# A cross-attention's values taken two units at a time, and the weight differences of an FFN moved beside the next attention's output products

## The reference

```python
# cross-attention, 16 heads, latents of width 32
C_q = Q @ Wq_d; C_kv = K @ Wkv_d
CqWqk = (C_q @ W_qk).reshape(b, n, H, LKV)
scores = einsum('bnhl,bkl->bhnk', CqWqk, C_kv) / sqrt(LKV)
attn = softmax(scores); V_up = (C_kv @ Wv_u).reshape(b, nkv, H, HD)
out = einsum('bhnk,bkhd->bnhd', attn, V_up)
# grouped attention: 32 heads of 128, 8 key heads, 16 blocks of 32 cached keys + 64 new ones
# FFN with weights in two values around a mean: for each of w1, w2, w3
d = w - base; coeff = mean(abs(d)); W = base + coeff * sign(d)
h = silu(x @ W1.T) * (x @ W3.T); out = h @ W2.T
x = x + xattn(ln(x)); x = x + attn(ln(x)); x = x + ffn(ln(x))
```

## Time and profile before

| | us |
|---|---|
| median of 3 runs | 906.02 (902.95 to 907.76) |
| the profiled execution | 903.59 |
| its span, first to last instruction | 901.8 |
| cross-attention's loop over contexts | 45.2 to 285.4 |
| rotated keys | 287.8 to 315.7 |
| grouped attention and FFN | from 317.6 |
| a group of the attention | 56.2 |
| busy: PE, DVE, ACT, POOL | 861.6, 609.3, 521.6, 416.4 |

### The profile page before, as it was taken

One profiled execution on the slowest core, in us unless ns is written; L12 is line 12 of the kernel. 1 busy time (PEld: TensorE's weight loads), 2 busy tenths in 40 slices (PEclk: granted clock), 3 DMA queues, 4 the chain that ended last, 5 costly groups with the idle time before them and its releaser, 6 DMA issues.

```text
span 901.8 us, 15515 instructions
## 1 busy us (share of the span) xinstructions
PE 861.6 (96%) x5402; PEld 654.4 (73%) x5402; DVE 609.3 (68%) x994; ACT 521.6 (58%) x1011; POOL 416.4 (46%) x272
## 2 busy tenths in 40 slices
PE   6899999999987979999999999999999999899998
PEld 4445555555532768888888888888888887788886
DVE  4865676577543448768587685876858769767784
ACT  4756666666675546546365463654636557555552
POOL 2597787778874024423244232442324525144430
PEclk9989999999998989999999999999999999999999
DMA  9947756532651522011020110201102004446521
GB/s 358 325 169 273 275 209 213 192 127 66 217 174 59 222 83 71 24 41 54 0 70 23 43 50 0 70 23 40 53 0 70 13 1 137 144 141 204 188 99 47
DMA packets 43202, 102.96 MB, mean 114 GB/s; under 512 B 7954, under 2 KB 13074, under 8 KB 42258
## 3 DMA queue, kind: packets, MB, share of 16 engines
q1 hardware_dynamic: 42866, 102.06, 33.0%
q10 hardware_dynamic: 288, 0.26, 0.1%
HBM read 96.95 MB, written 1.05 MB: 109 GB/s over the span
## 4 chain that ended last, share of the span: by engine, by line
PE 61%; DVE 2%; ACT 1%; DMA 1%; POOL 0%; SPq 0%; issue 0%
PE psum L1359 11%; PE psum L1345 10%; PE psum L1475 9%; PE psum L1413 8%; PE psum L1371 6%; PE psum L1489 4%; PE psum L1398 3%; PE psum L1389 3%; PE psum L1394 3%; PE psum L1380 1%; PE psum L1392 1%; PE psum L1390 1%; DMA ffn_raw<-in_L_ffn_mean_w_dram 1%; POOL ffn_quant L1860 0%; DVE x L1831 0%; DVE norm_stats L162 0%
## 5 line engine op out<-in xcount | busy, mean ns | idle before, releaser
L1847 POOL TENSOR_TENSOR head_probs<-head_probs,inverse_den 128x576 f32<-128x576 f32 x128 | 147.4, 1152 | 273.1 <-DVE inverse_den L1700 273.0
L982 DVE TENSOR_REDUCE max_part<-psum 128x1 f32<-128x804 f32 x128 | 121.0, 989 | 44.0 <-PE psum L694 43.9
L871 ACT ACTIVATE probs<-psum 128x512 f32<-128x512 f32 (+1 forms) x208 | 107.9, 601 | 54.7 <-PE psum L715 48.1
L1582 ACT ACTIVATE head_probs<-psum,neg_max 128x576 f32<-128x576 f32 x128 | 94.8, 741 | 51.1 <-DVE neg_max L1713 50.4
L555 POOL TENSOR_TENSOR prob_sums<-probs 128x1024 f32<-128x1024 f32 x48 | 114.2, 2389 | 18.7 <-ACT probs L871 9.8
L1713 DVE TENSOR_REDUCE neg_max<-psum 128x1 f32<-128x576 f32 x128 | 96.9, 757 | 23.8 <-PE psum L1359 22.6
L1359 PE MATMUL psum<-k_high,query_t_high 128*128 (+1 forms) x256 | 86.6, 338 | 2.0 <-DVE coeff L1786 2.0
L1693 DVE TENSOR_TENSOR probs_t_low<-psum,probs_t_high 128x512 fp32r<-128x512 f32 x124 | 84.8, 684 | 1.0
L715 PE MATMUL psum<-q_t,c_t 97*128 97x512 f32 (+1 forms) x208 | 73.7, 435 | 7.9 <-ACT probs L871 6.3
L1371 PE MATMUL psum<-ident,head_probs 128*128 128x128 f32 x496 | 77.9, 273 | 1.6 <-DVE query_t_low L1672 1.4
L694 PEld LDWEIGHTS psum<-c_t,q_t 96*128 96x128 f32 x256 | 43.6, 190 | 47.9 <-DVE max_part L982 25.1
(11 more groups left out here) (221 smaller groups left out, 1919.3 us busy)
## 6 DMA issues: line engine op xcount, KB each, us to landing
ctx_t_odd<-in_ctx_dram SPq DMA_DIRECT2D x4, 3202.0 KB, 10.7
w_raw<-in_L_ffn_w_dram SPq DMA_DIRECT2D x24, 448.0 KB, 5.1
w_raw<-in_L_ffn_mean_w_dram SPq DMA_DIRECT2D x24, 448.0 KB, 6.4
ffn_raw<-in_L_ffn_w_dram SPq DMA_DIRECT2D x42, 256.0 KB, 3.8
ffn_raw<-in_L_ffn_mean_w_dram SPq DMA_DIRECT2D x42, 256.0 KB, 4.3
cache<-in_ctx_dram SPq DMA_DIRECT2D x3, 3202.0 KB, 10.8
wq_nat<-in_L_attn_wq_dram SPq DMA_DIRECT2D x32, 256.0 KB, 3.0
wo_nat<-in_L_attn_wo_dram SPq DMA_DIRECT2D x32, 256.0 KB, 2.7
```

The costliest lines, as they stand in the source:

```text
L871: act.activation(prob_buffer(b, t)[0:rows, half * BANK:(half + 1) * BANK], psum[0:rows, n % SCORE_BANKS, :], ACT.Exp, scale=XSCALE).then_i ...
L982: dve.tensor_reduce(max_part[:, qt, pair:pair + 1], psum[:, bank:bank + 2, 0:PIECE_KEYS], AX.XY, ALU.max).then_inc(s_max, 1)
L1582: act.activation(probs[:, qt, :].rearrange("p (a k) -> p a k", a=2), psum[:, 2 * (qt % 2):2 * (qt % 2) + 2, 0:HALF], ACT.Exp, bias=neg_max ...
L1847: pool.tensor_tensor(probs[:, qt, :], probs[:, qt, :], rden[:, qt:qt + 1].to_broadcast([P, KEYS]), ALU.mult).then_inc(s["norm"], 1)
```

## The change

- The ring `probs` has eight tiles instead of four. `values` takes two units in one visit (16 records), so there are three visits of full tiles per context instead of six, after the scores of tiles 5, 9 and 12.
- Instead of six pair sums there are three sums of four or five tiles in contexts 0 to 4 (`STEADY`), five in contexts 5 and 6, and five sums and two single tiles in context 7. GpSimd adds tile by tile, ten additions a context in the first form. The tail's values are made in the same round as the denominators of the first sum, after the next context's first two tiles of scores.
- Maxima 14 and 15 follow the last visit of values, ahead of the compression and the turn of the maxima. Maximum 1 comes behind the scores of tile 3.
- The differences for `coeff` leave cross-attention. In the grouped attention, each group g from 1 to 7 handles a seventh of each matrix (1024 columns): six loads of 512 KB issued on SyncE's queue in its iteration for g, three differences on GpSimd in head (g, 0) behind the copy of the values, three absolute sums on ScalarE in head (g, 0) behind `output_weight_high(g, 0)`, one small addition on GpSimd in head (g, 1). The product that spreads the sums, and `coeff`, move into head (7, 2). `difference(0)` moves ahead of the first head.

```diff
-PIECE = WSIZE // P // BATCH
+PIECE = WSIZE // P // (NKV - 1)
...
+STEADY = ((0, 1, 2, 3), (4, 5, 6, 7), (8, 9, 10, 11, 12))
+FEWER = ((0, 1, 2), (3, 4, 5), (6, 7), (8, 9), (10, 11, 12))
+FEWEST = ((0, 1, 2), (3, 4), (5, 6), (7, 8), (9, 10), (11,), (12,))
+GROUPED = (STEADY,) * (BATCH - 3) + (FEWER, FEWER, FEWEST)
...
-            def add_pair(b, u):
...
+            def add_tile(b, t, n, first):
+
+                rows = slice(0, rows_of(t))
+                total = sum_buffer(b, n)
+                pool.wait_ge(s_exp, HALVES * b + 2 * t + 2)
+                if first:
+                    wait(pool, s_den, sum_freed(b, n))
+                else:
+                    pool.wait_ge(s_add, adds_through(b, t) - 1)
+                pool.tensor_tensor(total[rows, :], (prob_buffer(b, t - 1) if first else total)[rows, :],
+                                   prob_buffer(b, t)[rows, :], ALU.add).then_inc(s_add, 1)
...
+            def values(b, units):
+
+                pe.wait_ge(s_exp, HALVES * b + 2 * tiles_of(units[-1])[-1] + 2)
+                if units[0] == 0:
+                    pe.wait_ge(s_cnat, b + 1)
+                    wait(pe, s_u, 2 * b)
+                for u in units:
+                    for half in range(2):
+                        cols = slice(half * BANK, (half + 1) * BANK)
+                        for odd, t in enumerate(tiles_of(u)):
+                            at = 2 * LKV * half + LKV * odd
+                            mm = pe.matmul(psum[at:at + LKV, U_BANK, :], c_nat[:, b % 3, t, :],
+                                           prob_buffer(b, t)[:, cols], start=(u == 0), stop=(t + 2 >= KT))
...
+                pe.wait_ge(s_exp, HALVES * (b + 1))
+                pe.wait_ge(s_add, adds_through(b, parts[0][-1]))
+                for half in range(2):
+                    at = 2 * LKV * half
+                    mm = pe.matmul(psum[at:at + LKV, U_BANK, :], c_nat[0:TAIL, b % 3, KT - 1, :],
+                                   prob_buffer(b, KT - 1)[0:TAIL, half * BANK:(half + 1) * BANK], start=False, stop=True)
+                    add_up(0, 1, half)
+                mm.then_inc(s_pv, 1)
+                for n in range(1, len(parts), 2):
+                    wait(pe, s_add, adds_through(b, parts[n + 1][-1]))
                     for half in range(2):
...
+                maximum(0)
+                scores(b, 2)
+                if b == 0:
+                    maximum(1)
+                    compress(2)
+                scores(b, 3)
+                if b > 0:
+                    maximum(1)
+                    mix(b - 1)
+                maximum(2)
+                if b == 0:
+                    natural(2)
+                scores(b, 4)
+                maximum(3)
+                scores(b, 5)
+                maximum(4)
+                values(b, range(0, 2))
+                for t in range(6, 10):
+                    maximum(t - 1)
+                    scores(b, t)
+                maximum(9)
+                values(b, range(2, 4))
+                for t in range(10, KT):
+                    maximum(t)
+                    scores(b, t)
+                maximum(KT)
+                values(b, range(4, 6))
+                maximum(KT + 1)
+                maximum(KT + 2)
                 if b + 3 < BATCH:
                     compress(b + 3)
                 if lead:
                     turn_max(b + 1)
-                values(b, UNITS - 1)
                 if b + 3 < BATCH:
                     natural(b + 3)
                 if lead:
                     scores(b + 1, 0)
                     scores(b + 1, 1)
-                denominators(b)
+                tail_and_denominators(b)
```

In the grouped attention, SyncE's loop over g:

```diff
+                    if i == 1:
+                        sp.wait_ge(s_abs, 3 * (g - 1) + 1)
+                        for k in range(3):
+                            for j, n in enumerate(wnames[k]):
+                                sp.dma_start(pieces[k][:, j, :], flat[n][:, bass.ds((g - 1) * PIECE, PIECE)]
+                                             ).then_inc(s_piece[k], 16)
```

TensorE, in `score`, and ahead of the first head:

```diff
+                if isinstance(g, int) and n == NH - 2 and qt == 1:
+                    pe.wait_ge(s_tot, NKV)
+                    pe.matmul(psum[:, 3, HALF:HALF + 3], ones[:, :], total[:, :], start=True, stop=True).then_inc(s_all, 1)
+                elif isinstance(g, int) and n == NH - 2 and qt == 3:
+                    pe.wait_ge(s_co, 1)
...
-            pe.wait_ge(s_ones, 1)
-            pe.wait_ge(s_tot, 1)
-            pe.matmul(psum[:, 7, 0:3], ones[:, :], total[:, :], start=True, stop=True).then_inc(s_all, 1)
-            pe.wait_ge(s_co, 1)
             run(pe, head)
```

ScalarE, at the end of `head`:

```diff
                 if this and i == 0:
                     output_weight_high(g, i)
+                if last and i == 0:
+                    for k in range(3):
+                        abs_sum(g, k)
+
+            def abs_sum(g, k):
+
+                if k == 0:
+                    act.wait_ge(s_tot, g)
+                act.wait_ge(s_pdiff, 3 * (g - 1) + k + 1)
+                act.activation(pieces[k][:, 0, :], pieces[k][:, 0, :], ACT.Abs,
+                               accum_out=part[:, k:k + 1]).then_inc(s_abs, 1)
```

GpSimd, in `head`:

```diff
+                if i == 0 and last:
+                    pool.wait_ge(s["vl"], 2 * g + 2)
+                    for k in range(3):
+                        pool.wait_ge(s_piece[k], 32 * g)
+                        pool.tensor_tensor(pieces[k][:, 0, :], pieces[k][:, 0, :], pieces[k][:, 1, :],
+                                           ALU.subtract).then_inc(s_pdiff, 1)
```

More of the change, by code:

```diff
@@ L327, with adds_of, adds_before, adds_through @@
 C_WIDTH = MAIN + TAIL
-DIFF_AT = (0, 1, 2)
-ABS_AT = 3
+STEADY = ((0, 1, 2, 3), (4, 5, 6, 7), (8, 9, 10, 11, 12))
+FEWER = ((0, 1, 2), (3, 4, 5), (6, 7), (8, 9), (10, 11, 12))
+FEWEST = ((0, 1, 2), (3, 4), (5, 6), (7, 8), (9, 10), (11,), (12,))
+GROUPED = (STEADY,) * (BATCH - 3) + (FEWER, FEWER, FEWEST)
+def adds_of(b):
+    return [(t, n, t == tiles[1]) for n, tiles in enumerate(GROUPED[b]) for t in tiles[1:]]
+def adds_before(b):
+    return sum(len(adds_of(i)) for i in range(b))
+def adds_through(b, t):
+    done = [i + 1 for i, (at, n, first) in enumerate(adds_of(b)) if t == at or (first and t == GROUPED[b][n][0])]
+    return adds_before(b) + done[0] if done else 0
+def sum_number(b, n):
+    return sum(1 for i in range(b) for tiles in GROUPED[i] if len(tiles) > 1) + n
 COMPRESS_BANK = (4, 3, 6) + (4,) * (BATCH - 3)
@@ L619, in _ @@
             pool.wait_ge(s_rest, 5)
[L620 to L623, removed]
-                    add_pair(s, u)
-                    if s == 0 and u == 0:
+            for b in range(BATCH):
+                for t, n, first in adds_of(b):
+                    add_tile(b, t, n, first)
+                    if b == 0 and t == 1:
                         compressed_low(2)
-                add_tail(s)
-                if s + 3 < BATCH:
-                    compressed_low(s + 3)
+                if b + 3 < BATCH:
+                    compressed_low(b + 3)
         @block.tensor
@@ L1264, in attention_and_ffn @@
     total = core.sb("abs_total", [P, 3], ctx=own)
+    part = core.sb("abs_part", [P, 3], ctx=own)
+    pieces = [over(f"w_piece{k}", [P, 2, PIECE], F32, "cache", 8 * k * PIECE) for k in range(2)]
+    pieces.append(core.sb("w_piece2", [P, 2, PIECE], ctx=own))
+    s_piece = [core.sem(f"w_piece_in{k}", own) for k in range(3)]
+    s_pdiff = core.sem("w_piece_diff_done", own)
+    s_abs = core.sem("w_piece_abs_done", own)
     coeff = core.sb("coeff", [P, 3], ctx=own)
@@ L1848, in head @@
                                        ALU.mult).then_inc(s["norm"], 1)
+                if i == 1 and last and not (isinstance(g, int) and g == 0):
+                    pool.wait_ge(s_abs, 3 * g + 1)
+                    pool.tensor_tensor(total[:, :], total[:, :], part[:, :], ALU.add).then_inc(s_tot, 1)
                 if i == 0:
@@ L1867, in _ @@
             pool.wait_ge(core.cache_in, 2 * TOPK * 16)
+            pool.wait_ge(s["wql"], 2)
+            difference(0)
             run(pool, head)
```

151 lines of the change are left out of this document (48 added, 103 removed).

## The result

The changed kernel takes 922.64 us (median of four runs, 919.89 to 923.61) against 905.42 (902.95 to 907.76) before: a ratio of 1.019, 95% interval 1.015 to 1.022, so 17 us slower. Predicted were 927, with 908 to 938 as the range. The profiled execution took 919.89 us with a span of 917.8; the one before had 903.59 and 901.8.

A forecast was written before the change was run, and what follows sets the result against it. PE, busy 96% of the span, was taken as the bound. Terms -1.4 (context loop), +3.4 (its clock), -3.9, +0.3, +15.4 and +7.1 sum to +20.9 us on 903.6, giving 924.5; by the median 927, range 908 to 938.

The forecast's parts named there:

- Beside the output products: Grouped attention: three absolute sums on ACT delay PE's third turn 2.2 us in seven groups, +15.4 us; loads and differences hidden.
- The clock in the groups: Falls to 1.2 GHz behind the new 2.2 us waits, 1.7 us each, taken at 60%: +7.1 us, bounds 0 and 11.9.
- Middle contexts: Cross-attention loop: 2.9 us of PE work spared against 2.9 us of new waits, +0.1 us per context.
- Contexts 5 and 6: Cross-attention without compression: uncovered maxima make waits at turn and scores, +1.8 us each, 3.6; clock falls +3.4 for both.
- Contexts 0 and 7: First and last cross-attention contexts: less PE work and fewer holds behind POOL, -2.5 us and -2.9 us.
- Start of the attention: Coefficient wait of 1.97 us and small product go, -2.25; the low-clock spell behind it goes, -1.7; total -3.9 us.
- the first difference: Start of attention: 3.5 us on POOL ahead of its first normalisation; probabilities are wanted a head later, so costs nothing.
- Rival B: Groups: absolute sums cost PE nothing, hidden under the output products; 901.0 us, or 904.4 with clock falls; chance 0.14.
- the 0.26 us: Groups: PE's slack before its third turn; for sums to cost nothing, ACT must reach the turned copy by 391.5.

The follow-up runs named there:

- sums_spread: Changed kernel with the first two absolute sums of a group ahead of the output weight's copy, the third in the next head; 907.12 us, ratio 1.002.
- four_sums: Changed kernel with a fourth absolute sum, its result unused, beside the three behind the output weight's copy; 940.84 us, ratio 1.042.
- maxima_early: Changed kernel with each maximum one place earlier in PE's context loop from the second visit on; 917.04 us, ratio 1.013.
- loop_of_before: Changed kernel's grouped attention with the context loop of the kernel before, without its pieces of FFN weights; 921.44 us, ratio 1.018.
- combined_late: combined with one wait more: GpSimd starts the moved difference only after VectorE's low part of the values; 898.74 us, ratio 0.993.
- combined: Changed kernel with the edits of sums_spread and maxima_early, and the first FFN difference moved behind the values of group 0; 902.71 us, ratio 0.999.
- one_sum_behind: sums_spread with the third absolute sum back behind the output weight's copy; 907.38 us, ratio 1.003.

## Why the prediction was right

**Beside the output products: right in place and size.** Predicted 2.2 us in each of seven groups by the serial chain copy, three sums, turned copy, low part, third turn. Measured: groups of 58.4 against 56.2, the wait of 2.04 to 2.06 us seven times. sums_spread shows it by removal, four_sums by addition. Differences and loads were hidden, as assumed.

**The clock in the groups: the term that was most mis-sized.** A fall behind the new wait does occur, but I took 60% of seven falls, 7.1 us; the changed kernel's profiled execution had one of seven, 1.55 us (59.95 against 58.4). Over the three profiled kernels with the wait of 2.05 us four of 21 fell, and six of seven with 3.2 us. Both gaps of 1.97 and 1.98 us in the trace of before had been followed by a fall, and I carried that over as a likelihood; two cases were too few for it. The Trainium skill ("TensorE: Matmul & The Clock Gate", "HAM oscillation — how this bites in real kernels") tells of a kernel whose waits, each about 3 to 5 us, made every tile start at the low level. I carried that over to waits of 2.2 us, shorter than those of the page; these runs agree with it nearly at 3.2 us (6 of 7) and not at 2.05 (4 of 21).

**Middle contexts: the difference right, both of its terms too large.** +0.1 predicted, +0.2 measured. The prediction had 2.9 us of PE work spared and 2.9 us of new waits; the table has 1.7 us less busy time and 1.9 more without work (28.10 of 30.54 against 29.83 of 30.35). The waits stand where I put them (0.70 at the head, 0.72 at the compression, 0.70 and 0.22 at the next scores), the first of them shorter than its 1.1 us. That two errors of more than 1 us cancel is luck.

**Contexts 5 and 6: right.** 3.6 us of work and waits and 3.4 of clock predicted for the two together; 6.3 measured, of which half of 3.4 us at the low level, 1.7, is the clock in each. maxima_early shows the cause.

**Contexts 0 and 7: the sums right, their parts not all.** -2.5 and -2.9 predicted; -2.8 and -2.7 measured. But the prediction did not part the new order with its ring of eight from the pieces that left; loop_of_before shows that in context 7 the order makes 0.6 us and the pieces 2.1, and in context 0 0.7 and 1.4, with 0.7 by the clock of the execution.

**Start of the attention: a term with a wrong step.** -3.9 predicted, -1.0 measured (first outputs 94.25 us behind the last mix, 95.26 before). The step that failed is "PE no longer waits 1.97 us for the coefficient": below that wait lay another that it hid. After, in PE's order of time:

```profile
324.59 0.40 PE L1401 MATMUL psum<-k_high,query_t_high 128*128 128x288 f32 x1 [1.41 <-DVE query_t_low L1721]
```

This product stands 39.84 us behind the last mix, and stood 40.51 behind it: 0.67 us went, with the small product and its end, and not 2.25. Up to the next long wait's end, at 332.92 (333.98 before), another 0.88 went; the fall of the clock behind 325.1 had been priced at 1.7, and at the full clock PE now waits 0.45 us for ACT there. And the first difference, which I had costed at nothing, cost half a microsecond:

```profile
325.37 3.48 POOL L1916 TENSOR_TENSOR ffn_raw<-ffn_raw 128x1536 f32<-128x1536 f32 x1 [7.50 <-DVE wq_t_low L1717]
...
336.86 0.63 PE L1413 MATMUL psum<-ident,head_probs 128*128 128x128 f32 x4 [0.59 <-DVE probs_t_low L1742]
```

I had looked at when the first probabilities are wanted. But the copy of the values stands behind them in GpSimd's queue, VectorE's low parts behind that, and PE's third turn waits 0.59 us for these; combined_late, with the difference behind the values, has no such wait. What the difference does to a subtraction on DVE beside it, if it is moved there without a wait, the trace of before did not show and combined did.

**The sum.** 20.9 predicted, 16.0 between the spans, which are 0.5 up to the last mix, -1.0 to the first output, and 16.5 behind it. Predicted were 2.0, -3.9 and 22.8. The 6.3 us forecast too much behind the first output are the clock (7.1 against 1.55) and small change. At the start of the attention 2.9 us too much gain was forecast, and this error has the other sign; so the sum is nearer to the measurement than its terms are, and that too is luck. Of the 1.5 forecast too much up to the last mix, 1.2 is that it began at 43.94 us instead of 45.16; in the profiled executions of all kernels here it began anywhere from 43.2 to 45.7, so that is more likely the execution than the change. Rival B, that the sums lie under the products, is nearly what the program could have had: it fell by the place of a few lines. It could not have had all three there, since the third difference ends behind the copy's start; and the 0.26 us at which B was to be decided is too small, as one_sum_behind shows with a cover of 0.8 to 0.9.

## What to carry to other kernels

Idle time of an engine hides new work only where the engine's program puts that work ahead of what ends the idling; three sums behind a copy cost 15 us, two of them ahead of it and the third in the next head nothing. Before counting a removed wait as a gain, look for the next one below it, and before moving an elementwise operation to GpSimd's gaps, look at what VectorE does with two inputs in SBUF at that moment. Compare stretches of equal work and not whole spans: in context 0, length times granted clock told 1.4, 0.7 and 0.7 us apart, where the bare lengths would have given the pieces 0.3 and the order 2.5.

## What the runs showed of the hardware

**VectorE held up beside GpSimd.** Beside a GpSimd subtraction of 3.46 us a VectorE subtraction with both inputs in SBUF took 3.94 us instead of 0.68, and ended 0.55 us behind it; in combined_late, where it was over before GpSimd's began, it took 0.69. GpSimd's took 3.46 and 3.50 us, so it lost nothing by it. VectorE's additions with one input in PSUM kept their 0.69 us beside GpSimd's piece differences. The Trainium skill, "SBUF — State Buffer", section "Who interferes with whom", states this: a VectorE instruction with two SBUF inputs contends with a GpSimd instruction that reads SBUF. These rows agree.

**The clock.** Falls counted in the twelve profiled executions, all to 1.2 GHz: behind PE's wait of 2.05 us in the groups in 4 of 21 cases, of 3.2 us in 6 of 7; in contexts 5 and 6, with a wait of 1.83 and one of 1.20 us and 1.1 us of work between them, in 8 of 8, and with only the 1.20 in 0 of 8; at a wait of 2.4 to 3.0 us ahead of the first queries in 10 of 12. In two of the 8 (context 5 of sums_spread and of four_sums) the fall begins 0.4 and 0.3 us behind the 1.83 and ahead of the 1.20, so the second wait is not needed for it. Most of these falls lasted 3.4 us, three of them 6.8. Each execution has others too, one of 10.2 us that ends in context 0 and one or more between the last context and the attention. What decides whether a wait of 2 us is followed by a fall stays open: the order of work is the same in the groups that had one and in those that had none.
